# Two moves in VectorE's order inside an attention slot: V's low half goes behind the scaling of P, the rotation's sum in front of it

## The reference

```
q = (x @ wq).reshape(B, S, N_Q_HEADS, HEAD_DIM)
k = (x @ wk).reshape(B, S, N_KV_HEADS, HEAD_DIM)
v = (x @ wv).reshape(B, S, N_KV_HEADS, HEAD_DIM)
q = _rope(q, pos)
k = _rope(k, pos)
scores = jnp.einsum('bqhgd,bshd->bhgqs', qg, k) * sm_scale
allowed = (j <= i) & (j > i - SLIDING_WINDOW)
attn = jax.nn.softmax(jnp.where(allowed, scores, neg), axis=-1)
out = jnp.einsum('bhgqs,bshd->bqhgd', attn, v).reshape(B, S, N_Q_HEADS * HEAD_DIM)
return out @ wo
```

## Time and profile before

| | us |
|---|---|
| median of 3 runs | 747.13 (746.68 to 747.5) |
| the profiled execution | 746.33 |
| its span, first to last instruction | 744.6 |
| PE busy | 717.2 |
| VectorE busy | 601.0 |
| ScalarE busy | 413.3 |
| GpSimd busy | 396.5 |

### The profile page before, as it was taken

One profiled execution on the slowest core, in us unless ns is written; L12 is line 12 of the kernel. 1 busy time (PEld: TensorE's weight loads), 2 busy tenths in 40 slices (PEclk: granted clock), 3 DMA queues, 4 the chain that ended last, 5 costly groups with the idle time before them and its releaser, 6 DMA issues.

```text
span 744.6 us, 13949 instructions
## 1 busy us (share of the span) xinstructions
PE 717.2 (96%) x3692; PEld 603.1 (81%) x3692; DVE 601.0 (81%) x2060; ACT 413.3 (56%) x1122; POOL 396.5 (53%) x466
## 2 busy tenths in 40 slices
PE   8899789999999999999999999999999999998998
PEld 5787667888888888888888888888888888887786
DVE  6898778877887888878887888788878887788795
ACT  3324475657655676556655766576656665754320
POOL 0674268634864477438653765367535863462420
PEclk9999999999999999999999999999999999999999
DMA  8240003100220022002200120013000310030002
GB/s 266 73 158 16 0 3 98 43 1 2 73 70 1 0 70 70 0 0 70 56 14 0 56 70 14 0 32 94 15 0 0 99 28 1 1 114 1 0 31 85
DMA packets 25843, 32.13 MB, mean 43 GB/s; under 512 B 5833, under 2 KB 14281, under 8 KB 25298
## 3 DMA queue, kind: packets, MB, share of 16 engines
q1 hardware_dynamic: 25232, 30.69, 13.1%
q10 hardware_dynamic: 578, 1.05, 0.4%
HBM read 27.54 MB, written 4.19 MB: 43 GB/s over the span
## 4 chain that ended last, share of the span: by engine, by line
PE 70%; DVE 20%; issue 5%; ACT 3%; DMA 1%; POOL 1%; DVEq 0%; SPq 0%; ACTq 0%
PE bank L1102 26%; PE bank L1160 19%; PE bank L1145 6%; PE bank L1124 5%; PE bank L1068 5%; PE bank L1132 3%; DVE prob L822 2%; DVE rot L787 2%; DVE oT_lo L834 2%; DVE prob L814 1%; DVE sm L807 1%; PE bank L1121 1%; DVE rot L778 1%; ACT prob L550 1%; DVE pT_hi_lo L828 1%
## 5 line engine op out<-in xcount | busy, mean ns | idle before, releaser
L368 POOL TENSOR_TENSOR swap<-swap,rope 128x512 f32<-128x512 f32 x80 | 110.1, 1377 | 129.8 <-ACT swap L523 129.8
L550 ACT ACTIVATE prob<-sm,nmax 128x128 f32<-128x128 f32 x128 | 51.5, 403 | 151.4 <-DVE prob L814 150.4
L375 POOL TENSOR_SCALAR_AFFINE_SELECT pT_hi_lo<-pT_hi_lo 128x256 fp32r<-128x256 f32 x128 | 52.3, 409 | 140.3 <-DVE pT_hi_lo L828 139.8
L523 ACT ACTIVATE swap<-bank 64x512 f32<-64x512 f32 x160 | 94.9, 593 | 10.6 <-PE bank L1102 6.7
L558 ACT ACTIVATE pT_hi_lo<-bank 128x256 fp32r<-128x256 f32 x128 | 48.9, 382 | 71.5 <-PE bank L1132 50.6
L822 DVE TENSOR_SCALAR prob<-prob,rinv 128x128 f32<-128x128 f32 x256 | 83.3, 367 | 4.5
L385 POOL TENSOR_TENSOR q_lo<-rot,q_hi 128x512 fp32r<-128x512 f32 x64 | 82.6, 1291 | 6.9 <-ACT q_hi L531 6.9
L1160 PE MATMUL bank<-wo_hi,oT_hi 128*128 128x512 f32 x256 | 74.6, 413 | 5.0 <-DVE x L841 5.0
L828 DVE TENSOR_TENSOR pT_hi_lo<-bank,pT_hi_lo 128x256 fp32r<-128x256 f32 x128 | 53.6, 418 | 29.4 <-ACT pT_hi_lo L558 29.2
L1102 PE MATMUL bank<-xnT_hi,wq_hi 128*128 128x512 f32 x256 | 71.4, 391 | 2.2 <-DVE v_lo L798 1.4
L1102 PE MATMUL bank<-xnT_lo,wq_hi 128*128 128x512 f32 x256 | 73.4, 389 | 0.0
(11 more groups left out here) (150 smaller groups left out, 1768.9 us busy)
## 6 DMA issues: line engine op xcount, KB each, us to landing
raw<-in_L_attn_wq SPq DMA_DIRECT2D x32, 256.0 KB, 3.0
raw<-in_L_attn_wo SPq DMA_DIRECT2D x32, 256.0 KB, 2.6
x<-in_L_attn_x SPq DMA_DIRECT2D x4, 512.0 KB, 7.3
raw<-in_L_attn_wk SPq DMA_DIRECT2D x8, 256.0 KB, 2.7
raw<-in_L_attn_wv SPq DMA_DIRECT2D x8, 256.0 KB, 2.6
out<-x SPq DMA_DIRECT2D x8, 256.0 KB, 2.0
raw<-in_L_ffn_W_base ACTq DMA_DIRECT2D x4, 256.0 KB, 5.1
wb_keep_hi<-q_hi SPq DMA_DIRECT2D x1, 1024.0 KB, 4.9
```

The source lines that it names most:

```text
L368: nc.gpsimd.tensor_tensor(w, w, tab, ALU.mult).then_inc(t2_done, 1)
L523: last = nc.scalar.activation(swap[a:a + half, m % 2, :], A[m % 2][b:b + half, :], ACT.Copy)
L550: last = nc.scalar.activation(prob[:, s % 2, lo:hi], src, ACT.Exp, bias=nmax[:, s % 2, i:i + 1], scale=-1.0, accum_out=rsum[:, s % 2, i:i ...
```

## The change

In the body of a slot on VectorE three steps trade places. `rope_sum` is written ahead of `softmax_norm`, and `v_lo`, which slot 0 alone has, is written behind it and no longer at the head of the slot. The last half of all keeps its own place for `v_lo`. No other engine's order changes, and no instruction or transfer is added or taken away.

```diff
@@ -862,15 +862,15 @@
                         split, m = (ENDS.get(c) if not (last and hf == 1) else None for c in (s - 1, s))
-                        if s == 0 and not (last and hf == 1):
-                            v_lo(2 * g + hf, hf)
                         if s % G == 3 and not start:
                             x_add(beta - 1, (b - 1) % BATCH, 0)
                         if s % G == 0 and not (first and b < 2):
                             x_add(beta - 2, (b - 2) % BATCH, 1)
-                        softmax_norm(u, s)
                         if split is not None and split < 5:
                             rope_sum(2 * g + hf + 1, split)
+                        softmax_norm(u, s)
+                        if s == 0 and not (last and hf == 1):
+                            v_lo(2 * g + hf, hf)
                         if m is not None and m < 5:
                             rope_cos(2 * g + hf + 1, m)
```

## The result

The changed kernel takes **762.51 us** (median of 5 runs, 761.69 to 764.09), the kernel before 747.1 us (median of 5 runs beside it, 746.62 to 747.5). The ratio is 1.0213, with a 95% interval of 1.0202 to 1.0225: 15.4 us slower. I had predicted 759.5 us, that is 12.4 us slower, with an own range of 755 to 762 and a wide one of 752 to 768.5. The measured median lies 0.5 us above my own range and inside the wide one. The sign, the place and the mechanism were right; 3 us are missing from the sum.

What follows compares the result with a forecast made beforehand. The prediction took TensorE (PE), busy 717.2 of 744.6 us, as the bound. Its terms, -0.56 + 8.68 + 3.15 + 1.1 = +12.4 us, gave 759.5 us, with an own range of 755 to 762 and a wider one of 752 to 768.5.

Steps and rivals of the forecast that it cites:

- The sign, the place and the mechanism: Slower by 12.4 us, mainly in first-half slot 6 and second-half slot 0, where VectorE's scalings wait for POOL instructions.
- One reading of the chain: The chain that ended last goes back from `x_add` through VectorE to 343 us, slots 5 to 7 of the first half.
- Slot 6, 1.24 a pass: First half, passes 0 to 6: scalings wait for Wk's piece and POOL's next product; VectorE 1.24 us late, 8.68 in all.
- The rule on the port: VectorE and GpSimd block each other on SBUF ports; in slot 6 the port frees 0.13 us before VectorE's recorded end.
- `v_lo`, 0.45 a pass: Slot 0, second half: scalings wait for Wq's pieces, `v_lo` comes later, PE idles 0.45 us; 3.15 us over passes 0 to 6.
- Pass 0 and the last pass: First half of pass 0 gains 0.56 us in slot 0; the last pass loses 1.1 us through slot 6.
- is no term here: The granted clock is full throughout, so it adds nothing to the forecast.
- The near miss: Slot 2 and second halves' slot 6: POOL's product beats the second scaling in 21 places, 8.8 us, 768.3 us; chance 0.10.
- only a part is real: Only one of the stops in slot 6 and for `v_lo` counts, giving 750 to 756 us; chance 0.08.
- nothing is to be seen: Stops and gains cancel or slack takes them up, giving 747 us; chance 0.05.
- The faster case: Moved ahead in slot 6, `rope_sum` misses Wk's piece and cuts PE's wait for `x_add`, giving 741.9 us; chance 0.07.
- What I said of the profile: `x_add` stops some 1.9 us, `v_lo` stops some 7 times; first-half slot 6 scalings over 2 us, `rope_sum` about 0.9.

Runs made afterwards that it cites:

- e1: The kernel before with only `v_lo` moved behind the scalings, `rope_sum` left at its old place; 750.68 us, ratio 1.0048.
- e2: The kernel before with only `rope_sum` and `softmax_norm` swapped, `v_lo` left at its old place; 758.32 us, ratio 1.0153.
- e3: The changed kernel, but in slot 6 of the first half `rope_sum` stays behind the scalings; 750.38 us, ratio 1.0043 to the kernel before.
- e5: The changed kernel with POOL's piece of Wk made one slot later; 753.14 us, ratio 1.008 to the kernel before.
- e6: The changed kernel with one instruction in place of the two scalings of P; 749.17 us, ratio 1.0033 to the kernel before.
- e12: The changed kernel with both cures (Wk's piece one slot later, one scaling instruction) and two of Wo's four pieces half a slot earlier; 739.35 us.
- e4: The changed kernel, but `v_lo` keeps its old place in the second halves; 756.65 us, ratio 1.0134 to the kernel before.
- e10: The changed kernel with both cures: one scaling instruction and Wk's piece one slot later; 749.44 us, ratio 1.0033 to the kernel before.

## Why the prediction was nearly right

*The sign and the place.* One longer stop for `x_add` and a new one for `v_lo`, both through scalings that lose to POOL: e1 and e2 show them apart, e3 shows that slot 6 alone carries the first, and e5 and e6 that POOL's pieces and the number of VectorE instructions set its size. One reading of the chain was loose: it goes back through VectorE not to 343 us but to 339.8, with ScalarE's exponential in between, which is what the 14 us speak of.

*Slot 6, 1.24 a pass.* This term was right, with its mechanism. Measured 1.23 at `rope_cos`, and 1.25 in the length of a clean pass (e2: 78.82 against 77.57). Seven passes: 8.75 against 8.68.

*The rule on the port.* I had let the trace decide for a port that comes free 0.13 us before VectorE's recorded end. `rope_sum` ends at 197.75 and Wk's piece at 198.91, which is 1.16 later for an instruction of 1.28: the port was free some 0.12 before that end, as I took it. The Trainium skill (SBUF — State Buffer, "SBUF: two separate sides") has whichever starts first hold the pair of ports for the whole instruction, and the other fully blocked. That one blocks and does not share, the scalings of 2.37 and 0.48 us bear out; the end of the lock lies slightly ahead of the recorded one.

*`v_lo`, 0.45 a pass.* **This term was mis-sized**: 0.60 at the spot, 0.61 in the clean passes, 0.66 in e1. I took PE to follow 0.06 us behind `v_lo`'s end, from a row in which it did; it follows by 0.13 (210.34 to 210.47). And I left out that the first four matmuls behind a stop are longer, 1.18 us and not 1.07, though the 1.19 stood in the row that I took the 0.06 from the earlier trace rows. Seven passes: 4.3 us, not 3.15.

*Pass 0 and the last pass.* In pass 0 I had -0.56. V's high half is ready at 90.33 in the changed kernel, and the minimum starts at 91.08, 0.75 behind; before, it was 1.23 (90.25 against 89.02). That is -0.48: the scalings still run when V is ready, and `v_lo` starts 0.15 late. In the last pass I had 1.1: `o_lo` is 16.86 us later than before (673.84 against 656.98), the `x_add` of slot 6 18.16 (679.87, 661.71), and the last `x_add` but one 17.77 (711.86, 694.09), so 1.3 was lost and 0.4 given back: 0.9.

*The sum.* -0.48 + 8.75 + 4.3 + 0.9 = +13.5 us. The other 1.9 of the 15.4 stand beside **a step that the prediction didn't have**: it said that the clock "is no term here" because it was full throughout. That was misread: the trace of the kernel before has a granted 0.50 from 76.6 to 80.0 us, ahead of the head loop, behind a stop of PE of 2.15 us; only the head loop was free of it. And the prediction did not ask what its own longer stops would do to the clock. In the profiled runs, where the clock can be followed, the account closes: 764.09 - 746.33 = 17.8 us. The changed kernel is 1.3 us late before the head loop reaches V (88.45 to 89.75), where its trace has one more half-clock stretch, from 37.4; then come 13.5, and three times 1.0 for the stretches in the loop, together 17.8. How much of the 1.3 is that stretch stays open: e5 has the same two stretches there and is 0.66 late, e12 has one and is 0.93 late. For the medians the clock is argued and not shown, since the other runs have no trace. The one run of the changed kernel with a mean clock of 0.995 took 761.69 us, and runs of the kernel before with 0.995 took 747.08 to 747.55. So 14.1 to 14.6 of the 15.4 us are there at equal mean clock, and 13.5 of these are accounted for.

*The rivals.* The near miss (0.10) did not happen. That only a part is real (0.08) is refuted by e1 and e2, and that nothing is to be seen (0.05) by the result. The faster case (0.07) needed POOL's product 0.33 us sooner; at the predicted place it came late. e12 shows that its condition was the right one to name: with the product in time, and both cures, the new order is free. What I said of the profile was right but for two numbers. I gave the `x_add` stop as 1.9 us and it is 1.40, with 0.3 before it in the stop for P's low half. And I gave the stop for `v_lo` some 7 times: it comes in 4 passes, and is missing in the 3 that have a half-clock stretch.

## What to carry to other kernels

Before moving a VectorE instruction that works in SBUF alone, look up what POOL runs at the moment it comes up, and at each change-over behind it: every such instruction can lose once, so two short ones lose twice and one longer one once. And before moving a sum ahead of other work, look where the producer of its operand stands in the other engine's queue; the work it is moved past was what hid that wait. A stop of PE is not always worth only its length, since the clock may be lower behind it.

## What the runs showed of the hardware that I had not expected

- **PE at half clock behind a short stop.** In the changed kernel, three of seven passes have 3.4 us at a granted 0.50 (1.2 GHz), all beginning 0.1 to 1.3 us after PE resumes from 1.40 us of waiting for `x_add`, preceded by 0.30 for P's low half. The four other passes, with the same stop, kept 1.00. e2 and e4 had it in one pass of seven each. The kernel before, e1 and e3, whose stops for `x_add` are at most 0.7 us, had none in the head loop, nor had e6 and e10, whose stops for `x_add` are 1.4 us in pass 0 and 1.05 in the others. So in these traces it comes behind the longer stops and not each time. No run changed the length of the stop alone, and what decides in which pass was not tried.
- **A margin of a tenth of a microsecond holds.** In slot 2 the second of two scalings begins some 0.1 us before POOL's product and gets through, in all 21 places of the changed kernel's trace.
- **The single scaling is no shorter by itself** (0.42 us against 0.48 for the pair); it pays only because it stands in line for POOL once.
